# Attention and FFN with split fp32: four engines' order of work in front of the output projection

## The chip, the cores and the metric

The kernel runs on one core of one Trainium2 chip. The metric is device time in microseconds, the median of several executions. TensorE does the matrix products, ScalarE activations and copies, VectorE elementwise work, GpSimd some elementwise work and DMA issues, SyncE only DMA issues. Each runs its own list of instructions strictly in order and meets the others through semaphores.

## The reference

The input is `x` of 2048 rows by 1024 and a context of the same shape, seen as four batches (C = 4) of 512 rows (T = 512).

```python
def _L0_xattn_ref(query, key, value, mask, Wq, Wk, Wv, Wo):     # 32 query heads, 8 key/value heads, size 128
    q = (query @ Wq).reshape(b, t, h, d)
    k = (key @ Wk).reshape(b, t, kv_h, d)
    v = (value @ Wv).reshape(b, t, kv_h, d)
    q = apply_rope(q)
    k = apply_rope(k)
    logits = jnp.einsum('btkgd,bTkd->bkgtT', q, k) * ATTN_MULT
    logits = MAX_ATTN_VAL * jnp.tanh(logits / MAX_ATTN_VAL)
    logits = jnp.where(m, logits, -1e+30)
    weights = jax.nn.softmax(logits, axis=-1)
    attn = jnp.einsum('bkgtT,bTkd->btkgd', weights, v)
    return attn.reshape(b, t, h * d) @ Wo
...
x = x + xattn(_layernorm(x), ctx, ctx, mask, Wq, Wk, Wv, Wo)
x = x + ffn(_layernorm(x))                                      # base product, router with top 2 of 8, low-rank experts
```

The batches of the kernel's attention are the 16 sequences of 128 rows, four of them side by side in each c; a head group g is one of the 8 key/value heads with its four query heads.

## The kernel before, in words

Every fp32 operand of a large product is split into a high part of the type fp32r and a low part, and a product is three matmuls (helper `three`, lines 235 to 237): high by high, low by high, high by low. The split is one copy on ScalarE (the names end in `h`) and one subtraction on VectorE or GpSimd (names in `l`). The program has these stages, one behind the other: keys and values (K, V), queries (Q), attention with the output projection (O), and the feed-forward part. The last quarter of V (batch c = 3) is not projected in the K/V stage but in front of O, between the last query products and the first output products.

O is written as a schedule of steps `at`, from -16 to 255, eight steps for each of the 32 head groups `gi`. TensorE's `pe_att` (line 1257), ScalarE's `act_step` (1395), VectorE's `dve_step` (1494), GpSimd's `pool_step` (1580) and SyncE's `sp_step` (1687) each walk the steps, and in a step the order of the lines is the order on the engine. Tables say what falls into which step: `S_AT` scores, `DEN_AT` row sums, `ROWS_AT` the broadcast of reciprocals, `PV_AT` products of probabilities and values, `PL_AT` low parts of probabilities, `SPLIT` weight splits, `WL_AT` raw loads, `V_EVAC` copies of the value projection. Steps -16 to -1 are the front of O that this case is about; they lie at about 926 to 985 us.

The parts of one head group (four blocks b, numbered x = 4 gi + b):

- Query block x: `qf` is loaded by SyncE (`load_qk`), `qh` copied by ScalarE (`q_high2`, line 1374), `ql` subtracted by VectorE (`q_low2`, 1382). TensorE makes the scores of it; ScalarE applies tanh (1415), VectorE the mask's minimum (1545), ScalarE exp into `Pf` (1439) and the copy `Ph` (1441), VectorE the low part `Pl` (1567).
- Scores of block x write the same PSUM bank as those of x - 2, so they wait for exp of x - 2.
- Row sums: eight matmuls on ones (1300) into a bank, a copy `rT` (1393), a small transfer to `r` on 128 partitions (1604), the reciprocal on VectorE (1492), a small store to `rD` in DRAM (1588), and four broadcast loads into `RB` (1598), 256 KB each. The last three DMAs are issued by GpSimd.
- The product with the values waits for `Pl`. VectorE multiplies it by `RB` (1553), ScalarE copies it to `Ah` (1426) and VectorE forms `Al` (1512), which the output products read.

A weight piece x of 128 by 1024 comes from a raw load of SyncE (line 1198, three buffers), a copy `Rh` on ScalarE (1225) and a subtraction `Rl` on VectorE (1230) into a ring of four; here the pieces 8 to 11 are the value weights, and 12 and up the output weights. The last value projection consists of eight blocks of 24 matmuls. Its results are copied and split like everything else (`v_high`, line 1475, and `v_low`, 1481): blocks 0 to 3 into the upper halves of `Ah` and `Al`, which are free until the second head group, blocks 4 to 7 into two staging buffers `stg`. From there GpSimd stores them to `vE` in DRAM (`v_store`, 1488); they are read only by the last eight head groups.

Semaphores are counted per name: `tick` raises one, `wait_ge` waits for the value a named event reached; `SAME` lets names that never overlap share one.

Of the kernel before, what the change touches and what calls it, by code (L numbers as in the profile page):

```python
# [16 lines left out]
T = 512  # L17
# [38 lines left out]
SHARED_DMA += [(f"d_qw{i}", [f"d_ks{i}" if i < 2 else f"d_vs{i // 2 - 1}{i % 2}"]) for i in range(6)]  # L56
SHARED_DMA += [(f"d_vp{i // 2}{i % 2}", [f"d_vc{i // 2}{i % 2}"]) for i in range(4)]
SHARED_DMA += [(f"d_rb{i}", [f"d_bx{i}"]) for i in range(4)]
SHARED_DMA += [(f"d_x1{k}", [f"d_xt{k}"]) for k in range(4)]
SAME = {x: name for name, of in list(SHARED.items()) + SHARED_DMA for x in of}  # L60


# [35 lines left out]
def program(nc, xT, xN, ctxT, gran, mask, bias, cst, dram, out):  # L98
    kD, vD, vE, qD, XcD, QSD, X2D, x1D, rD = dram
    ctx = ExitStack()  # L100
    with ctx:
# [124 lines left out]
        def f(ap):  # L226
            return ap.bitcast(F32)
# [994 lines left out]
        def w_high(t, x):  # L1222
            w_free(t, x)
            t.wait_ge(f"d_w{raw_of(x)}", x)
            t.e.activation(piece(x)[1], raw[raw_of(x)][:, :], ACT.Copy).then_inc(*t.tick("w_hi", x))  # L1225
# [115 lines left out]
        def a_war(t, gi):  # L1341

            if gi > 1:
                t.wait_ge("o_job", 8 * (gi - 2) + 7)
            elif gi:
                for n in range(4):
                    for x in range(2):
                        t.wait_ge(f"d_vp{n % 2}{x}", n)
            else:
                t.wait_ge("q_pe", (31, 6))  # L1350

# [43 lines left out]
        def act_step(t, at):  # L1395
            e = t.e
            if at == -10:
                sums_copy(t, at)
            if at == -16:
                q_high2(t, 0)  # L1400
                q_high2(t, 1)
            if at not in (-9, -6, -2):
                v_high(t, at)
            for x in SPLIT.get(at, []):
                if x not in (7, 8, 9, 11, 12):
                    w_high(t, x)
            if at == -10:
                w_high(t, 11)
            if at == -9:
                v_high(t, at)  # L1410
            for gi, b in S_AT.get(at, []):
                x = 4 * gi + b
                s = ps[sbank[x % 2]][:, :]
                t.wait_ge("a_s", x)
                e.activation(s, s, ACT.Tanh, scale=SCALE / CAP).then_inc(*t.tick("a_tanh", x))  # L1415
                if at != -12:
                    q_high2(t, x + 2 if at != -11 else 4)
            if at == -13:
                w_high(t, 7)
            if at in (-3, 4):  # L1420
                sums_copy(t, -2 if at < 0 else at)
            for gi, b in PV_AT.get(at, []):
                x, i = 4 * gi + b, gi % 2
                t.wait_ge("a_an", x)
                a_war(t, gi)
                e.activation(Ah[:, 4 * i:4 * i + 4, b * P:b * P + P], v4(ps[obank[x % 2]][:, :]), ACT.Copy).then_inc(*t.tick("a_ah", x))  # L1426
            if at not in (-10, -2, 4):
                sums_copy(t, at)
            if at == -7:
                v_high(t, -6)  # L1430
            if at == -3:
                w_high(t, 12)
                v_high(t, -2)
            for gi, b in S_AT.get(at, []):
                x = 4 * gi + b
                s = ps[sbank[x % 2]][:, :]
                t.wait_ge("a_min", x)
                p_free(t, x)
                e.activation(Pf[x % NP][:, :], s, ACT.Exp, scale=CAP).then_inc(*t.tick("a_exp", x))  # L1439
                t.wait_ge("a_exp", x)  # L1440
                e.activation(Ph[x % NP][:, :], Pf[x % NP][:, :], ACT.Copy).then_inc(*t.tick("a_ph", x))
                if at == -13:
                    w_high(t, 8)
                if at == -11:
                    w_high(t, 9)
                    q_high2(t, 5)
            if 1 <= at < 9:
                n = at - 1
                t.wait_ge("o_job", n)
                t.wait_ge("v_job", ("last", 3))  # L1450
                e.activation(Y[:, n, :], ps[ring_bank(n)][:, :], ACT.Copy).then_inc(*t.tick("y_first", n))  # L1451
            act_ln(t, at)

        V_EVAC = {-9: (0, 1), -8: (2,), -7: (3,), -6: (4,), -4: (5,), -2: (6,), 0: (7,)}

        def v_key(n):
            return ("half", n) if n < 3 else ("quarter", 3) if n == 3 else ("full", n - 4) if n < 7 else ("last", 3)
# [16 lines left out]
                    t.wait_ge("q_pe", (31, 6))  # L1474
                e.activation(v_place(n)[:, 0, :], ps[v_bank(n)][:, :], ACT.Copy).then_inc(*t.tick("v_vh", n))

        def v_low(t, at):
            e = t.e
            for n in V_EVAC.get(at, []):
                t.wait_ge("v_vh", n)  # L1480
                e.tensor_tensor(v_place(n)[:, 1, :], ps[v_bank(n)][:, :], f(v_place(n)[:, 0, :]), ALU.subtract).then_inc(*t.tick("v_vl", n))

        def v_store(t, at):
            for n in V_EVAC.get(at, []):
                half, b4 = n // 4, n % 4
                t.wait_ge("v_vl", n)
                for x in range(2):
                    t.e.dma_start(vE[x, b4][:, T * half:T * half + T], f(v_place(n)[:, x, :])).then_inc(*t.tick(f"d_vp{n % 2}{x}", n, 16))

        def row_sums(t, gi):  # L1490
            t.wait_ge(f"d_rt{gi % 2}", gi)
# [2 lines left out]
        def dve_step(t, at):  # L1494
# [3 lines left out]
                q_low2(t, 1)  # L1498
            if at not in (-9, -4, -2):
                v_low(t, at)  # L1500
            for gi, b in S_AT.get(at - 1, []):
                if at not in (-12, -11, -10, -3, -2):
                    q_low2(t, 4 * gi + b + 2)
            if at == -9:
                w_low(t, 11)
                row_sums(t, 0)
                v_low(t, at)
            for gi, b in PV_AT.get(at - 1, []):
                x, i = 4 * gi + b, gi % 2
                t.wait_ge("a_ah", x)  # L1510
# [13 lines left out]
            if at >= 9:  # L1524
# [9 lines left out]
                else:  # L1534
                    t.wait_ge("y_first", m)
                e.tensor_tensor(Y[:, m, :], ps[ring_bank(n)][:, :], Y[:, m, :], ALU.add).then_inc(*t.tick("y_add", n))  # L1536
            for x in [y for y in SPLIT.get(at, []) if at < 0 and y not in (5, 7, 8, 9, 10, 11, 12)]:
                w_low(t, x)
            if at == -15:
                w_low(t, 5)  # L1540
# [15 lines left out]
                w_low(t, 7)  # L1556
            if at == -11:
                q_low2(t, 4)
                w_low(t, 9)
                q_low2(t, 5)  # L1560
            for x in [y for y in SPLIT.get(at, []) if at >= 0 and at != 4 or y in (8, 10)]:
                w_low(t, x)
            for gi, b in PL_AT.get(at, []):
                x = 4 * gi + b
                t.wait_ge("a_ph", x)
                t.wait_ge("a_den", gi)
                e.tensor_tensor(Pl[x % NP][:, :], Pf[x % NP][:, :], f(Ph[x % NP][:, :]), ALU.subtract).then_inc(*t.tick("a_pl", x))
            if at - 1 in DEN_AT and at not in (-9, 5):
                row_sums(t, DEN_AT[at - 1])
            if 11 <= at < 19:  # L1570
# [9 lines left out]
        def pool_step(t, at):  # L1580
# [18 lines left out]
            if at in DEN_AT:  # L1599
# [2 lines left out]
                if gi > 1:  # L1602
                    t.wait_ge(f"d_rs{gi % 2}", gi - 2)
                e.dma_start(r16[gi % 2][:, :], rT[gi % 2][0:P:32, :]).then_inc(*t.tick(f"d_rt{gi % 2}", gi, 16))  # L1604
            v_store(t, at)
            pool_rows(t, at)
            pool_ln(t, at)

# [78 lines left out]
        def sp_step(t, at):  # L1687
# [2 lines left out]
                load_qk(t, 1)  # L1690
            for x in WL_AT.get(at, []):
                w_load(t, x)
            if at == -9:
                load_v(t, 1)
            if at in (2, 3, 5, 6):
                j = (2, 3, 5, 6).index(at)
# [17 lines left out]
        for x in range(RAW + 4, 12 + 133):  # L1714
            at = split_at(x - RAW)
            if x - RAW >= 12 + 128:
                at = NT - 6 + 2 * (x - RAW - 140)
            WL_AT.setdefault(at + 1, []).append(x)


        def sp_att_early(t, u):
# [576 lines left out]
```

## Time and profile before

| | us |
|---|---|
| median of three runs | 2129.25 |
| lowest, highest | 2128.1, 2129.94 |
| the profiled execution's own time | 2128.13 |
| its span | 2126.3 |

| engine | busy us | share |
|---|---|---|
| TensorE, matmuls | 2118.6 | 100% |
| VectorE | 1652.2 | 78% |
| ScalarE | 879.3 | 41% |
| GpSimd | 338.8 | 16% |

The granted clock of TensorE is full throughout (the page's digits are all 9, the stretches say 1.00). A matmul is listed with a duration of 0.39 us, but they are pipelined: without a wait one starts every 0.23 us. So TensorE's time is read from the starts. Idle time of the other engines costs nothing unless TensorE comes to wait for them. Where the list of waits names an engine, it gives the one whose semaphore came last.

### The profile page before, as it was taken

To read this page: it belongs to the slowest core of one execution; us is meant where nothing else is said; L and a number is where in the kernel's file an instruction comes from. 1 tells how busy PE (TensorE), PEld (TensorE's weight loads), DVE (VectorE), ACT (ScalarE), POOL (GpSimd) and SP (SyncE) were. 2 spreads that over 40 slices of the span, in tenths; PEclk is the share of its full clock that TensorE was granted. 3 is DMA by queue.
4 is the path that set the end of the run, shared out by engine and by line. 5 is a ranking of instruction groups with operands and counts; after the bars stand their busy time and mean duration, and the time that the engine had idled before them with its cause. 6 is when DMAs were issued, how large, how long until landed. Compare 5 with 4: busy or idle time off the path is not lost.

```text
span 2126.3 us, 26531 instructions
## 1 busy us (share of the span) xinstructions
PE 2118.6 (100%) x9429; PEld 1721.3 (81%) x9429; DVE 1652.2 (78%) x2387; ACT 879.3 (41%) x1353; POOL 338.8 (16%) x438
## 2 busy tenths in 40 slices
PE   9999999999999999999999999999999999999999
PEld 8888888888888888877777877777787777888887
DVE  6969759999986666677877888998999898856533
ACT  3323343222241111157555556655666566423211
POOL 0000025666350000003111111111111110100000
PEclk9999999999999999999999999999999999999999
DMA  8778667777685566679656666678557854596761
GB/s 314 244 247 287 237 208 303 277 282 267 258 320 210 211 216 212 219 249 314 226 190 197 232 238 198 198 257 290 199 171 264 295 197 153 191 359 247 283 248 61
DMA packets 198820, 508.52 MB, mean 239 GB/s; under 512 B 20896, under 2 KB 46624, under 8 KB 196640
## 3 DMA queue, kind: packets, MB, share of 16 engines
q1 hardware_dynamic: 172448, 424.43, 56.6%
q0 software_dynamic: 26240, 82.38, 11.6%
q8 instruction: 76, 1.25, 0.2%
q14 instruction: 56, 0.46, 0.1%
HBM read 357.26 MB, written 149.16 MB: 238 GB/s over the span
## 4 chain that ended last, share of the span: by engine, by line
PE 97%; DMA 1%; ACT 1%; DVE 0%; issue 0%; SPq 0%; ACTq 0%; DVEq 0%
PE pq L235 32%; PE pq L236 31%; PE pq L237 31%; PE pq L1300 1%; PE pq L1959 0%; PE pq L1958 0%; DMA raw<-gran 0%; DMA raw<-ctxT 0%; DMA RB<-rD 0%; DMA rD<-r 0%; PE pq L411 0%; ACT Rh L1225 0%; SPq L1122 0%; DVE Rl L1230 0%; ACT Pf L1439 0%
## 5 line engine op out<-in xcount | busy, mean ns | idle before, releaser
L235 PE MATMUL pq<-Ah,Rh 128*128 128x512 f32 x1024 | 399.0, 390 | 0.0
L237 PE MATMUL pq<-Ah,Rl 128*128 128x512 f32 x1024 | 398.5, 389 | 0.0
L236 PE MATMUL pq<-Al,Rh 128*128 128x512 f32 x1024 | 398.5, 389 | 0.0
L235 PE MATMUL pq<-Xq,qW 128*128 128x512 f32 x896 | 348.7, 389 | 0.5 <-issue 0.4
L236 PE MATMUL pq<-Xq,qW 128*128 128x512 f32 x896 | 348.6, 389 | 0.0
L237 PE MATMUL pq<-Xq,qW 128*128 128x512 f32 x896 | 348.5, 389 | 0.0
L1230 DVE TENSOR_TENSOR Rl<-raw,Rh 128x1024 fp32r<-128x1024 f32 x176 | 214.2, 1218 | 91.4 <-ACT Rh L1225 91.0
L1225 ACT ACTIVATE Rh<-raw 128x1024 fp32r<-128x1024 f32 x176 | 185.3, 1054 | 166.2 <-PE pq L237 128.2
L235 PEld LDWEIGHTS pq<-Ah,Rh 128*128 128x128 f32 x1024 | 192.2, 188 | 41.9 <-ACT Y L1451 0.8
L237 PEld LDWEIGHTS pq<-Ah,Rl 128*128 128x128 f32 x1024 | 192.2, 188 | 40.5
L236 PEld LDWEIGHTS pq<-Al,Rh 128*128 128x128 f32 x1024 | 192.2, 188 | 40.1
L235 PEld LDWEIGHTS pq<-Xq,qW 128*128 128x128 f32 x896 | 168.2, 188 | 36.4 <-issue 1.3
L236 PEld LDWEIGHTS pq<-Xq,qW 128*128 128x128 f32 x896 | 168.2, 188 | 35.0
L237 PEld LDWEIGHTS pq<-Xq,qW 128*128 128x128 f32 x896 | 168.2, 188 | 34.6
L1536 DVE TENSOR_TENSOR Y<-pq,Y 128x512 f32<-128x512 f32 x248 | 169.4, 683 | 31.5 <-PE pq L237 31.2
L872 ACT ACTIVATE qW<-qraw 128x512 fp32r<-128x512 f32 x96 | 60.6, 632 | 293.3 <-PE pq L237 269.7
L1415 ACT ACTIVATE pq<-pq 128x512 f32<-128x512 f32 x128 | 74.6, 583 | 203.6 <-PE pq L237 203.5
L1604 POOL DMA_DIRECT2D r<-rT x32 | 22.6, 708 | 741.3 <-ACT rT L1393 718.3
L1545 DVE TENSOR_TENSOR pq<-pq,Bm 128x512 f32<-128x512 f32 x128 | 88.9, 695 | 64.9 <-ACT pq L1415 64.0
L1426 ACT ACTIVATE Ah<-pq 128x512 fp32r<-128x512 f32 x128 | 76.7, 599 | 94.3 <-DVE pq L1553 94.2
L235 PE MATMUL pq<-F,Rh 128*128 128x512 f32 x288 | 112.9, 392 | 0.0
L237 PE MATMUL pq<-F,Rl 128*128 128x512 f32 x288 | 112.2, 390 | 0.0
(243 smaller groups left out, 3935.2 us busy)
## 6 DMA issues: line engine op xcount, KB each, us to landing
raw<-gran SPq DMA_DIRECT2D x177, 512.0 KB, 4.4
QSD<-qW SPq DMA_DIRECT2D x64, 512.0 KB, 2.9
qD<-qt SPq DMA_DIRECT2D x128, 256.0 KB, 5.4
qW<-QSD SPq DMA_DIRECT2D x64, 512.0 KB, 3.4
qf<-qD SPq DMA_DIRECT2D x64, 512.0 KB, 6.1
RB<-rD POOLq DMA_DIRECT2D x128, 256.0 KB, 4.2
qraw<-gran SPq DMA_DIRECT2D x48, 512.0 KB, 5.2
kD<-kst SPq DMA_DIRECT2D x32, 512.0 KB, 5.7
```

Source lines behind the costliest of these rows:

```text
L235: e.matmul(dst, lh, rh, start=first, stop=False, skip_group_check=more)
L236: e.matmul(dst, lh, rl, start=False, stop=False, skip_group_check=more)
L237: return e.matmul(dst, ll, rh, start=False, stop=last, skip_group_check=more)
L872: e.activation(q_place(u)[:, 0, :], q_source(u), ACT.Copy).then_inc(*t.tick("q_hi", u))
L1225: t.e.activation(piece(x)[1], raw[raw_of(x)][:, :], ACT.Copy).then_inc(*t.tick("w_hi", x))
L1230: t.e.tensor_tensor(l, raw[raw_of(x)][:, :], f(h), ALU.subtract).then_inc(*t.tick("w_lo", x))
L1300: m = e.matmul(Tb[32 * y:32 * y + 32, :], f(ones[:, 0:32]), Pf[(4 * gi + y) % NP][:, :], start=True, stop=True, tile_position=(0, 32 * y))
L1415: e.activation(s, s, ACT.Tanh, scale=SCALE / CAP).then_inc(*t.tick("a_tanh", x))
L1426: e.activation(Ah[:, 4 * i:4 * i + 4, b * P:b * P + P], v4(ps[obank[x % 2]][:, :]), ACT.Copy).then_inc(*t.tick("a_ah", x))
L1536: e.tensor_tensor(Y[:, m, :], ps[ring_bank(n)][:, :], Y[:, m, :], ALU.add).then_inc(*t.tick("y_add", n))
L1545: e.tensor_tensor(v4(s), v4(s), bc(Bm[:, :].unsqueeze(1), [P, 4, P]), ALU.min).then_inc(*t.tick("a_min", x))
L1604: e.dma_start(r16[gi % 2][:, :], rT[gi % 2][0:P:32, :]).then_inc(*t.tick(f"d_rt{gi % 2}", gi, 16))
```

## The change

All of it is in the order of work in the steps -13 to -3.

- ScalarE: in step -10 the split of weight piece 11 moves behind the tanh and the query copy; in step -11 query copy 5 goes ahead of weight piece 9; value blocks 0 and 1 are copied in the order 1, 0.
- VectorE: the low part of query block 5 goes ahead of weight piece 9; weight piece 10 ahead of the minimum; weight piece 11 ahead of query block 6; and value block 0 is subtracted behind `Pl` 0, block 1 ahead of it.
- GpSimd: the stores of value blocks 0 to 3, which stood ahead of and behind the broadcast of the first head group, all move to step -3, behind the staging stores of blocks 4 and 5. They get semaphores of their own (`d_vf`, shared with `d_x1`), and the wait of `Ah` of the second head group (`a_war`) now names these.
- SyncE: raw loads 12, 13 and 14 move to the steps -7, -6 and -5, and the second value load from step -9 to step -5.

```diff
-SHARED_DMA += [(f"d_x1{k}", [f"d_xt{k}"]) for k in range(4)]
+SHARED_DMA += [(f"d_x1{k}", [f"d_xt{k}", f"d_vf{k // 2}{k % 2}"]) for k in range(4)]
...
@@ a_war
-                        t.wait_ge(f"d_vp{n % 2}{x}", n)
+                        t.wait_ge(f"d_vf{n % 2}{x}", n)
@@ act_step
-            if at == -10:
-                w_high(t, 11)
             if at == -9:
                 v_high(t, at)
             for gi, b in S_AT.get(at, []):
...
             if at == -13:
                 w_high(t, 7)
+            if at == -10:
+                w_high(t, 11)
...
                 if at == -11:
+                    q_high2(t, 5)
                     w_high(t, 9)
-                    q_high2(t, 5)
...
-        V_EVAC = {-9: (0, 1), -8: (2,), -7: (3,), -6: (4,), -4: (5,), -2: (6,), 0: (7,)}
+        V_EVAC = {-9: (1, 0), -8: (2,), -7: (3,), -6: (4,), -4: (5,), -2: (6,), 0: (7,)}
...
-        def v_low(t, at):
+        def v_low(t, at, which=range(8)):
             e = t.e
-            for n in V_EVAC.get(at, []):
+            for n in [x for x in V_EVAC.get(at, []) if x in which]:
@@ v_store
-                    t.e.dma_start(vE[x, b4][:, T * half:T * half + T], f(v_place(n)[:, x, :])).then_inc(*t.tick(f"d_vp{n % 2}{x}", n, 16))
+                    t.e.dma_start(vE[x, b4][:, T * half:T * half + T], f(v_place(n)[:, x, :])).then_inc(
+                        *t.tick(f"d_v{'p' if n > 3 else 'f'}{n % 2}{x}", n, 16))
@@ dve_step
+            if at == -9:
+                w_low(t, 11)
             for gi, b in S_AT.get(at - 1, []):
                 if at not in (-12, -11, -10, -3, -2):
                     q_low2(t, 4 * gi + b + 2)
             if at == -9:
-                w_low(t, 11)
                 row_sums(t, 0)
-                v_low(t, at)
+                v_low(t, at, (1,))
...
-            for x in [y for y in SPLIT.get(at, []) if at < 0 and y not in (5, 7, 8, 9, 10, 11, 12)]:
+            for x in [y for y in SPLIT.get(at, []) if at < 0 and y not in (5, 7, 8, 9, 11, 12)]:
                 w_low(t, x)
...
             if at == -11:
                 q_low2(t, 4)
+                q_low2(t, 5)
                 w_low(t, 9)
-                q_low2(t, 5)
...
                 e.tensor_tensor(Pl[x % NP][:, :], Pf[x % NP][:, :], f(Ph[x % NP][:, :]), ALU.subtract).then_inc(*t.tick("a_pl", x))
+            if at == -9:
+                v_low(t, at, (0,))
@@ pool_step
-            v_store(t, at)
+            if at > -7:
+                v_store(t, at)
+            if at == -3:
+                for x in (-9, -8, -7):
+                    v_store(t, x)
@@ sp_step
-            if at == -9:
+            if at == -5:
                 load_v(t, 1)
...
-            WL_AT.setdefault(at + 1, []).append(x)
+            WL_AT.setdefault({12: -7, 13: -6, 14: -5}.get(x, at + 1), []).append(x)
```

VectorE, steps -11 to -9, before. `Rl_169`, `Rl_170` and `Rl_171` are the low parts of weight pieces 9, 10 and 11, `ql_153` and `ql_152` those of query blocks 5 and 6, `Ah<-pq` those of value blocks 0 and 1, `Pl_185` that of the first probabilities:

```order
L1382 TENSOR_TENSOR ql_152<-qf_163,qh_150 128x512
L1230 TENSOR_TENSOR Rl_169<-raw_172,Rh_165 128x1024
L1382 TENSOR_TENSOR ql_153<-qf_163,qh_151 128x512
L1545 TENSOR_TENSOR pq<-pq,Bm 128x512
L1230 TENSOR_TENSOR Rl_170<-raw_173,Rh_166 128x1024
L1382 TENSOR_TENSOR ql_152<-qf_163,qh_150 128x512
L1230 TENSOR_TENSOR Rl_171<-raw_174,Rh_167 128x1024
L1492 RECIPROCAL r_55<-r_55 128x16
L1481 TENSOR_TENSOR Ah<-pq,Ah 128x512 x2
L1567 TENSOR_TENSOR Pl_185<-Pf_192,Ph_178 128x512
L1481 TENSOR_TENSOR Al<-pq,Al 128x512
```

The same place on VectorE in the changed kernel:

```order
L1382 TENSOR_TENSOR ql_152<-qf_163,qh_150 128x512
L1382 TENSOR_TENSOR ql_153<-qf_163,qh_151 128x512
L1230 TENSOR_TENSOR Rl_169<-raw_172,Rh_165 128x1024
L1230 TENSOR_TENSOR Rl_170<-raw_173,Rh_166 128x1024
L1547 TENSOR_TENSOR pq<-pq,Bm 128x512
L1230 TENSOR_TENSOR Rl_171<-raw_174,Rh_167 128x1024
L1382 TENSOR_TENSOR ql_152<-qf_163,qh_150 128x512
L1493 RECIPROCAL r_55<-r_55 128x16
L1481 TENSOR_TENSOR Ah<-pq,Ah 128x512
L1569 TENSOR_TENSOR Pl_185<-Pf_192,Ph_178 128x512
L1481 TENSOR_TENSOR Ah<-pq,Ah 128x512
L1481 TENSOR_TENSOR Al<-pq,Al 128x512
```

Query block 5 moved ahead of weight piece 9, piece 10 ahead of the minimum, piece 11 ahead of query block 6, and `Pl_185` between the two value blocks.

GpSimd, first head group, before (`r_55` and `r_56` belong to head groups 0 and 1):

```order
L1604 DMA r_55<-rT_154 128x1x16
L1588 DMA rD<-r_55 128x16
L1488 DMA vE<-Ah 128x512 x4
L1598 DMA RB<-rD 128x512 x4
L1488 DMA vE<-Al 128x512 x4
L1488 DMA vE<-stg_176 128x512 x2
L1488 DMA vE<-stg_177 128x512 x2
L1604 DMA r_56<-rT_155 128x1x16
```

The same place on GpSimd in the changed kernel:

```order
L1608 DMA r_55<-rT_154 128x1x16
L1592 DMA rD<-r_55 128x16
L1602 DMA RB<-rD 128x512 x4
L1488 DMA vE<-stg_176 128x512 x2
L1488 DMA vE<-stg_177 128x512 x2
L1488 DMA vE<-Ah 128x512 x4
L1488 DMA vE<-Al 128x512 x4
L1608 DMA r_56<-rT_155 128x1x16
```

The four broadcasts now follow the store of the reciprocals directly, and the eight stores of `Ah` and `Al` stand together ahead of the small transfer of the second head group.

SyncE, raw loads 9 to 14 with the loads of head groups 1 and 2 among them, before (`qf_162` and `kT_146` are of head group 2):

```order
L1198 DMA raw_174<-gran 128x1024
L1198 DMA raw_172<-gran 128x1024
L1657 DMA qf_162<-qD 64x4x512 x2
L1662 DMA kT_146<-kD 64x2x512 x2
L1198 DMA raw_173<-gran 128x1024
L1678 DMA vT_149<-vD 128x2x512
L1198 DMA raw_174<-gran 128x1024
```

The same place on SyncE in the changed kernel:

```order
L1198 DMA raw_174<-gran 128x1024
L1665 DMA qf_162<-qD 64x4x512 x2
L1670 DMA kT_146<-kD 64x2x512 x2
L1198 DMA raw_172<-gran 128x1024
L1198 DMA raw_173<-gran 128x1024
L1198 DMA raw_174<-gran 128x1024
L1686 DMA vT_149<-vD 128x2x512
```

Queries and keys of head group 2 moved ahead of a raw load, and the value load behind the last of three.

## Rows read from the trace of the kernel before

**Rows 1.** The page, busy time of TensorE: us, share of the span, instructions.

```profile
PE 2118.6 (100%) x9429; PEld 1721.3 (81%) x9429; DVE 1652.2 (78%) x2387; ACT 879.3 (41%) x1353; POOL 338.8 (16%) x438
```

**Rows 2.** Waits of TensorE: waited for, us in total, times, longest.

```profile
PE pq L235 <- ACT Pf L1439: 1.4, 1, 1.4
PE pq L235 <- DVE ql L1382: 1.0, 1, 1.0
```

**Rows 3.** Two stretches: length, busy us (instructions) by engine, clock, DMA share, GB/s.

```profile
960.00:980.00 20.00, 18.63 (x85) 14.01 (x84) 12.59 (x22) 11.14 (x21) 8.35 (x16) 1.00 1.02 366
1020.00:1820.00 800.00, 800.00 (x3602) 635.98 (x3601) 706.25 (x1071) 485.95 (x763) 110.34 (x196) 1.00 0.65 218
```

**Rows 4.** Timeline of TensorE, steps -9 and -8: start, duration, instruction, idle before.

```profile
952.27 0.40 PE L237 MATMUL pq<-qh,kT 128*128 128x512 f32 x1
953.69 0.50 PE L235 MATMUL pq<-qh,kT 128*128 128x512 f32 x1 [1.02 <-DVE ql L1382]
954.03 0.39 PE L236 MATMUL pq<-ql,kT 128*128 128x512 f32 x1
...
958.38 0.39 PE L237 MATMUL pq<-Rh,Vl 128*128 128x512 f32 x1
958.81 0.50 PE L235 MATMUL pq<-Rh,Vh 128*128 128x512 f32 x1
```

**Rows 5.** Timeline of TensorE, step -3.

```profile
975.34 0.47 PE L235 MATMUL pq<-Ph,vT 128*128 128x512 f32 x1
975.65 0.40 PE L236 MATMUL pq<-Pl,vT 128*128 128x512 f32 x1
975.88 0.40 PE L237 MATMUL pq<-Ph,vT 128*128 128x512 f32 x1
977.65 0.47 PE L235 MATMUL pq<-qh,kT 128*128 128x512 f32 x1 [1.37 <-ACT Pf L1439]
```

**Rows 6.** Timeline of ScalarE around query block 5.

```profile
950.74 1.04 ACT L1225 ACTIVATE Rh<-raw 128x1024 fp32r<-128x1024 f32 x1
951.68 0.61 ACT L1374 ACTIVATE qh<-qf 128x512 fp32r<-128x512 f32 x1
```

**Rows 7.** Timeline of VectorE, the first reciprocal.

```profile
958.67 0.24 DVE L1492 RECIPROCAL r<-r 128x16 f32<-128x16 f32 x1
```

**Rows 8.** Timeline of GpSimd, the small transfer.

```profile
953.09 0.71 POOL L1604 DMA_DIRECT2D r<-rT  x1 [317.52 <-ACT rT L1393]
```

**Rows 9.** DMA issues, 950 to 972 us: count, KB each, median us to landing.

```profile
vE<-stg POOLq DMA_DIRECT2D x2, 256.0 KB, 9.0
r<-rT POOLq DMA_DIRECT2D x1, 8.0 KB, 4.8
```

**Rows 10.** Chain that ended last, 959 to 972 us: start, us, what.

```profile
959.21 5.64 DMA rD<-r
...
965.25 5.83 DMA RB<-rD
...
971.18 0.71 DVE pq L1553
```

**Rows 11.** DMA issues, whole run.

```profile
RB<-rD POOLq DMA_DIRECT2D x128, 256.0 KB, 4.2
...
r<-rT POOLq DMA_DIRECT2D x32, 8.0 KB, 2.3
rD<-r POOLq DMA_DIRECT2D x32, 8.0 KB, 3.7
```

**Rows 12.** Timeline of GpSimd's DMA issues, 968 to 982 us.

```profile
968.55 2.15 POOL L1488 DMA_DIRECT2D vE<-Al  x4
...
976.09 1.07 POOL L1488 DMA_DIRECT2D vE<-stg  x2 [4.33 <-DVE stg L1481]
981.12 0.71 POOL L1604 DMA_DIRECT2D r<-rT  x1 [3.96 <-ACT rT L1393]
```

**Rows 13.** Timeline of VectorE, the second head group's reciprocal.

```profile
989.41 0.24 DVE L1492 RECIPROCAL r<-r 128x16 f32<-128x16 f32 x1
```

More of the change, by code:

```diff
@@ L1558, in dve_step @@
                 q_low2(t, 4)
+                q_low2(t, 5)
                 w_low(t, 9)
-                q_low2(t, 5)
-            for x in [y for y in SPLIT.get(at, []) if at >= 0 and at != 4 or y in (8, 10)]:
+            for x in [y for y in SPLIT.get(at, []) if at >= 0 and at != 4 or y == 8]:
                 w_low(t, x)
```

## The prediction

> **What bounds the kernel now.** I read the page first, then the list of waits of TensorE, then stretches, then single instructions of the stretch that waits. The page has TensorE busy for 2118.6 of 2126.3 us [rows 1]. The change leaves its instructions and their order alone, so it can only give back what TensorE waits. In the list of waits there is little: 1.4 us for ScalarE's `Pf`, 1.0 us for VectorE's `ql` [rows 2]; what else it waits stands at the start and end of the program, which the change does not touch. A stretch of 800 us in the long stage O has 800.00 us of TensorE work, while 960 to 980 us has 18.63 of 20, with a DMA share of 1.02 [rows 3]. The granted clock is 1.00 in both, so it is no term.
>
> Where TensorE does not wait, a matmul starts every 0.23 us (975.65, 975.88 in [rows 5]); three make 0.68, six 1.36, twenty-four 5.44. A late start also costs the restart after it, which the list of waits does not count. Place one: the scores that start at 953.69 could have started at 952.27 + 0.23 = 952.50, 1.19 us sooner, and the next matmul comes 0.34 instead of 0.23 later, 0.11 more: **1.30 us**. Place two: the value projection steps from 958.38 to 958.81, 0.43 instead of 0.23, and I count the same 0.11 of restart: **0.31 us** [rows 4]. Place three: scores at 977.65 which could have followed 975.88 at 976.11, 1.54 and some 0.08 of restart: **1.62 us**. A fourth is too short for the list: 975.34 to 975.65 is 0.31, a restart of **0.08 us** behind a wait for `Al` [rows 5]. Together 3.31 us, the ceiling of a gain in this profiled execution.
>
> **Edit by edit.** Nothing is added or removed: the same activations, subtractions and transfers in another order.
>
> *Query before weight on ScalarE and VectorE (steps -11 to -9).* In place one TensorE waits for `ql` 5 (the low part of the sixth query block), whose high part ran on ScalarE only at 951.68, behind the weight copy `Rh` 9 of 0.94 us started at 950.74 [rows 6]. Swapped, `qh` 5 runs 950.74 to 951.3 and `ql` 5 (0.60 us) ends by 951.95, before 952.50. The 1.30 us goes. What is moved behind: `Rh` 9 ends at 952.2, `Rl` 9 (1.13 us) by 953.45; TensorE, now 1.3 us earlier, wants it at 952.50 + 0.68 + 1.36 = 954.54. `Rl` 10 goes ahead of a minimum: by 954.9, wanted at 955.90. `Rh` 11 now stands behind a tanh and a query copy, about 954.7 to 955.7, so `Rl` 11 ends about 956.95. It used to end just ahead of the reciprocal at 958.67 [rows 7], which is place two. TensorE wants it at 957.26. So the 0.31 us goes too, with 0.3 us of margin; at worst it stays.
>
> *The first reciprocal.* The row sums' small transfer leaves at 953.09 and takes 4.8 us [rows 8, 9]: it lands near 957.9, while VectorE came to the reciprocal at 958.67 because it was at work. Now `ql` 6 ends by 957.5, so the reciprocal runs at 958.0, 0.65 us earlier. Then value low part 1, `Pl` 0 and low part 0, 0.60 apart from 958.15: `Pl` 0 is there at 959.4, wanted at 957.26 + 1.36 + 0.68 = 959.30. I count 0.1 us of new wait. Ten operations of 0.60 from 959.35 close low part 4 at 965.35, wanted at 959.4 + 0.68 + 5.44 = 965.5: nothing. Were the small transfer 1 us slower, 1 us would be lost here; faster, the 0.1 goes.
>
> *Broadcast before stores on GpSimd.* This is place three. Its chain: `rD` 5.64 us from 959.21, `RB` 5.83 us from 965.25, product at 971.18 [rows 10], then in ScalarE's order `Ah`, a staging copy, tanh and exp up to 977.5. From the broadcast's landing (971.08) to the scores (977.65) are 6.57 us. GpSimd's issue of the four `Ah` stores costs nothing there, since it was over before `rD` landed; what they cost is in flight: 1 MB on the same queue ahead of `RB`, with the DMA engines full. Over the whole run `rD` takes 3.7 us and `RB` 4.2 us at the median [rows 11]. In the new order the four stores are gone, and SyncE's `qf` and `kT` (1.5 MB) are issued before a raw load that waits for `Rl` 9, instead of behind it. Between the two pairs (5.64 and 5.83; 3.7 and 4.2) I take 4.2 and 4.7, nearer to the median because both crowds leave. Issue of `rD` 958.55, landed 962.75; `RB` issued 963.15, landed 967.85; scores possible at 974.4. TensorE without its waits comes to them at 976.11 - 1.30 - 0.31 - 0.08 + 0.1 = 974.5. So all 1.62 us goes, without margin. Bounds: with the medians there is 0.9 us to spare; with the old pair the broadcast lands at 970.4 and the scores start at 977.0, a gain of 0.7 in all.
>
> Here the Trainium skill has a formula (DMA: Bandwidth & Descriptors, Anatomy of one DMA): about 2.0 us fixed plus bytes over 436 GB/s. By it `rD` would take 2.0 us and `RB` 2.6 us, and place three would be cleared with some 4 us to spare. The rows disagree on the size, 5.64 and 5.83 here and 3.7 and 4.2 at the median, so it is no part of the sum.
>
> *Value stores and raw loads later.* Eight stores of 256 KB now leave in one go behind a pair of staging stores. That pair stood at 976.09 and comes 3.2 us earlier with the broadcast: 972.9 to 973.95, and the eight, 0.54 us each, until 978.3. Behind them on GpSimd is the next head group's small transfer, at 981.12 before [rows 12]; its producer is 3.1 us earlier too, so it leaves at 978.3 instead of 978.0. Its reciprocal ran at 989.41 [rows 13], so it must land by 986.3: 8.0 us of room against 4.8 above. The new wait for these stores is at the next group's product copies, some 20 us later. The raw loads wait for their buffers anyway and are wanted after 978; the value load behind them later still. All free.
>
> Sum: 1.30 + 0.31 + 1.62 + 0.08 - 0.1 = 3.2; less 0.1 for the place without margin: **3.1 us**. The profiled execution took 2128.13 us (2126.3 of span and 1.8 around it): it becomes 2125.0. The median of the runs is 1.1 us above it, and I forecast in its terms: 2129.25 - 3.1 = **2126.1 us**. Behind about 1000 us everything is only shifted.
>
> **Rivals.**
> B, *the broadcast is as slow as before*: SyncE's loads made it slow, not the stores. For it: the DMA share of 1.02, and three raw loads and `vT` still fall between 953.5 and 958. Against: 1 MB of stores and 1.5 MB of queries leave. Gain 0.7: 2128.5.
> C, *the weights become the wait*: `Rh` 11 slips behind the tanh, which waits for TensorE; `Rl` 11 is late and the chain from the reciprocal with it. Place two stays and 0.6 us come on top: 1.30 + 1.62 + 0.08 - 0.6 - 0.3 of a place three not fully cleared = 2.1: 2127.2. For it: 0.3 us of margin only.
> D, *the stores hold back the next group's row sums*, the slow side. Before, four `Al` and two staging stores were issued from 968.55 [rows 12], and the last pair, issued until 971.2, took 9.0 us [rows 9]: 11.7 us for six, 1.9 us each. Ten from 972.9 at that pace end at 991.9, and the small transfer, behind them on the queue, 2.3 us (its median, [rows 11]) later at 994.2, not by 986.3: 7.9 us late, with VectorE standing in the reciprocal and the weights behind it. -3.1 + 7.9 = +4.8: 2134.1. It decides once the transfer takes 8.0 us from its issue, and is slower than before from 11.1 us on. Against it: that pace was measured among SyncE's loads, with two broadcasts in flight.
> For D the Trainium skill has a rule (same page, Two DMAs through the same engine are not ordered): descriptors of one queue start in order. By that rule the small transfer does stand behind the large ones; whether it must wait for their end no row of before shows.
>
> **How the numbers follow.** Forecast 0.60, B 0.20, C 0.13, D 0.07 (slower by over 0.2% in 0.04 of it). The forecast's own range is 2.6 to 3.3 us of gain, and about 0.8 us either way for the median of a few runs (three spread from 2128.1 to 2129.94): 2125.0 to 2127.4. For 8 in 10 I take in B and C, to 2128.8, and below 2124.7. 0.2% is 4.3 us, about what can be told from no change; it lies above the ceiling of 3.3. It is reached only if other executions wait a microsecond longer here than the profiled one, as their 1.1 us more would allow: faster 0.16, same 0.80, slower 0.04.
>
> **What would show it.** TensorE's list of waits without `ql` and `Pf`; scores at 952.5 and 974.5; `qh` 5 ahead of `Rh` 9; the first product on `RB` by 968.0 (after 969.5 B is right); `Rl` 11 ended by 957.2, or C; the second reciprocal near 986.3 and no gap of TensorE there, or D. I am wrong if TensorE waits over 0.5 us between 985 and 1030, or if the time moves by over 4.3 us.

## The result and the profile after

| | before, us | after, us |
|---|---|---|
| median (22 runs each, side by side) | 2129.44 | 2126.31 |
| lowest, highest | 2128.05, 2131.89 | 2124.47, 2131.09 |
| the profiled execution's own time | 2128.13 | 2125.62 |
| its span | 2126.3 | 2123.8 |

The ratio is 0.9985, with a 95% interval of 0.9979 to 0.9992: a gain of 3.1 us, with 1.7 and 4.5 as its ends. That is under 0.2%, as forecast, and the time is 0.2 us above the predicted one.

In this document "to the third row sums" is the time from the first row-sum matmul of head group 0 (L1300) to that of head group 3. It holds all that the change touches and nothing of the program's start. Before it is 1024.65 - 950.71 = 73.94 us, after 1022.15 - 951.53 = 70.62 us, **3.32 us** less. Behind that point the program is only shifted: from the row sums of head group 3 to the end of the span are 1101.65 us before and after (1101.65 to 1101.73 in all ten traces). The span shrank by 2.5 only, because the first row sum itself comes 0.82 us later in this execution, 951.53 instead of 950.71; that is made in the keys and values at the very start, which the change doesn't touch, and differs from one execution to the next (950.51 to 952.23 in the ten traces). So 0.8 us is to be taken off a time of after when it is set beside one of before.

TensorE's busy time on the page of after; it answers to [rows 1]:

```profile
PE 2118.4 (100%) x9429; PEld 1721.7 (81%) x9429; DVE 1653.3 (78%) x2387; ACT 879.0 (41%) x1353; POOL 337.7 (16%) x438
```

TensorE's list of waits, after (waited for, us in total, times, longest); it answers to [rows 2]:

```profile
PE pq L411 <- DVE sel L516: 1.5, 1, 1.5
PE pq L235 <- issue: 0.4, 1, 0.4
PE pq L235 <- DVE kRl L522: 0.2, 1, 0.2
```

`Pf` and `ql` are gone, and nothing took their place: of the three left, `sel` and `kRl` belong to the program's start and the 0.4 us to the query stage, ahead of the change. Two stretches, after, answering to [rows 3]:

```profile
960.00:980.00 20.00, 20.00 (x93) 15.62 (x92) 15.26 (x25) 14.09 (x26) 9.24 (x17) 1.00 0.83 288
1020.00:1820.00 800.00, 800.00 (x3602) 635.99 (x3601) 706.53 (x1071) 485.71 (x762) 110.54 (x197) 1.00 0.65 218
```

TensorE now fills 20 of 20 us in place of 18.63. The stage behind is what it was. TensorE's timeline, after, at the places one, two and three and at the one late start left; it answers to [rows 4, 5]:

```profile
953.09 0.39 PE L237 MATMUL pq<-qh,kT 128*128 128x512 f32 x1
953.32 0.40 PE L235 MATMUL pq<-qh,kT 128*128 128x512 f32 x1
...
957.87 0.39 PE L237 MATMUL pq<-Rh,Vl 128*128 128x512 f32 x1
958.10 0.39 PE L235 MATMUL pq<-Rh,Vh 128*128 128x512 f32 x1
...
974.87 0.39 PE L237 MATMUL pq<-Ph,vT 128*128 128x512 f32 x1
975.10 0.39 PE L235 MATMUL pq<-qh,kT 128*128 128x512 f32 x1
...
1000.45 0.39 PE L237 MATMUL pq<-Ah,Rl 128*128 128x512 f32 x1
1000.85 0.47 PE L235 MATMUL pq<-Ph,vT 128*128 128x512 f32 x1
1001.16 0.39 PE L236 MATMUL pq<-Pl,vT 128*128 128x512 f32 x1
```

The scores that waited follow at 0.23 us (953.32 and 975.10), and so does the value projection of place two (958.10, the seventh of the block's eight threes of matmuls, as 958.81 was before). The one late start left is 1000.85: 0.17 late and 0.08 of restart, 0.25 us. The same matmul was late before, in a place that the prediction didn't count:

```profile
1003.08 0.39 PE L237 MATMUL pq<-Ah,Rl 128*128 128x512 f32 x1
1003.36 0.47 PE L235 MATMUL pq<-Ph,vT 128*128 128x512 f32 x1
1003.66 0.39 PE L236 MATMUL pq<-Pl,vT 128*128 128x512 f32 x1
```

That is 0.05 late and 0.07 of restart, 0.12 us.

ScalarE and VectorE, after, answering to [rows 6, 7, 13]. In the first of two fences ScalarE has query block 5 ahead of the weight piece, and the exp for which place three waited:

```profile
951.45 0.61 ACT L1374 ACTIVATE qh<-qf 128x512 fp32r<-128x512 f32 x1
951.97 1.04 ACT L1225 ACTIVATE Rh<-raw 128x1024 fp32r<-128x1024 f32 x1
...
973.71 0.60 ACT L1439 ACTIVATE Pf<-pq 128x512 f32<-128x512 f32 x1
```

VectorE has the first reciprocal, `Pl` 0, the first product on `RB`, and the second reciprocal:

```profile
958.31 0.25 DVE L1493 RECIPROCAL r<-r 128x16 f32<-128x16 f32 x1
...
959.03 0.68 DVE L1569 TENSOR_TENSOR Pl<-Pf,Ph 128x512 fp32r<-128x512 f32 x1
...
967.98 0.70 DVE L1555 TENSOR_TENSOR pq<-pq,RB 128x512 f32<-128x512 f32 x1 [1.56 <-DMA RB<-rD]
...
986.20 0.24 DVE L1493 RECIPROCAL r<-r 128x16 f32<-128x16 f32 x1
```

VectorE still waits 1.56 us for `RB`, but the product is at 967.98 instead of 971.18. exp ends at 974.31, and the scores start at 975.10. Before, exp ended at 977.5 and the scores started 0.15 later; so they could have started at 974.46 here, and there is a margin of 0.6 us in this execution.

GpSimd's issues, after, answering to [rows 8, 10, 12]:

```profile
953.80 0.71 POOL L1608 DMA_DIRECT2D r<-rT  x1 [317.44 <-ACT rT L1393]
958.86 0.56 POOL L1592 DMA_DIRECT2D rD<-r  x1 [4.35 <-DVE r L1493]
964.54 2.15 POOL L1602 DMA_DIRECT2D RB<-rD  x4 [5.13 <-DMA rD<-r]
...
973.34 1.07 POOL L1488 DMA_DIRECT2D vE<-stg  x2 [5.55 <-DVE stg L1481]
974.40 2.13 POOL L1488 DMA_DIRECT2D vE<-Ah  x4
976.52 2.13 POOL L1488 DMA_DIRECT2D vE<-Al  x4
978.64 0.70 POOL L1608 DMA_DIRECT2D r<-rT  x1
```

How long these took to land, after (count, KB each, median us), from three windows: 953 to 968, the first broadcast alone, and 970 to 980 us. They answer to [rows 9, 10]:

```profile
r<-rT POOLq DMA_DIRECT2D x1, 8.0 KB, 4.5
rD<-r POOLq DMA_DIRECT2D x1, 8.0 KB, 5.4
...
RB<-rD POOLq DMA_DIRECT2D x1, 256.0 KB, 3.3
...
r<-rT POOLq DMA_DIRECT2D x1, 8.0 KB, 7.0
```

`rD` is hardly faster than before (5.4 against 5.64). The first `RB` is: 3.3 against 5.83. And the second group's small transfer, 8 KB behind ten stores, took 7.0 us: 978.64 + 7.0 = 985.64, while VectorE's order reaches the reciprocal at 986.20. That is a margin of 0.56 us.

### The profile page after: what moved, and what is told of

It is laid out like the page before. It is cut to its first block, busy times and chain, and to the rows that moved or that the text cites. A ratio compares the mean times of both kernels' runs of the same rounds, so it can differ in the third digit from the quotient of the medians.

```text
span 2123.8 us, 26535 instructions
## 1 busy us (share of the span) xinstructions
PE 2118.4 (100%) x9429; PEld 1721.7 (81%) x9429; DVE 1653.3 (78%) x2387; ACT 879.0 (41%) x1353; POOL 337.7 (16%) x438
## 4 chain that ended last, share of the span: by engine, by line
PE 99%; DMA 0%; DVE 0%; SPq 0%; ACT 0%; issue 0%
PE pq L235 32%; PE pq L236 32%; PE pq L237 32%; PE pq L1300 2%; PE pq L1967 0%; PE pq L1966 0%; DMA kraw<-ctxT 0%; SPq L687 0%; PE pq L432 0%; PE pq L1773 0%; PE pq L1774 0%; PE pq L433 0%; PE pq L1989 0%; PE pq L1982 0%; DVE Xl L522 0%; ACT Xh L476 0%
```

## The experiments

The question behind them: which of the three engines' edits brings the gain, do they add up, and how near is the slow side? "ADDITIVE" and "COUPLED" are two theories of how the places add up. "STORES" and "LOADS" name what made the broadcast slow. "QUEUE" and "FREE" say whether a small transfer waits for the stores ahead of it on its queue or not.

| kernel | to third row sums | less before | median | before beside it | ratio (95%) |
|---|---|---|---|---|---|
| before | 73.94 | | | | |
| after | 70.62 | -3.32 | 2126.31 | 2129.44 | 0.9985 (0.9979 to 0.9992) |
| e1: ScalarE's and VectorE's edits alone | 74.99 | +1.05 | 2129.79 | 2129.09 | 1.0004 (0.9995 to 1.0013) |
| e2: GpSimd's edit alone | 72.15 | -1.79 | 2128.23 | 2129.09 | 0.9999 (0.9990 to 1.0008) |
| e3: SyncE's edit alone | 73.79 | -0.15 | 2128.52 | 2129.09 | 0.9997 (0.9988 to 1.0006) |
| e4: all but SyncE's edit | 70.71 | -3.23 | 2126.20 | 2129.09 | 0.9987 (0.9978 to 0.9996) |
| e5: eight stores twice | 79.59 | +5.65 | 2135.15 | 2129.21 | 1.0029 (1.0018 to 1.0040) |
| e6: raw loads later still | 74.56 | +0.62 | 2129.73 | 2129.21 | 1.0005 (0.9995 to 1.0014) |
| e7: stores behind the small transfer | 72.50 | -1.44 | 2127.00 | 2129.21 | 0.9993 (0.9984 to 1.0002) |
| e8: e6 and e7 together | 77.94 | +4.00 | 2132.45 | 2129.21 | 1.0016 (1.0007 to 1.0025) |

Differences of under 2 us don't show in the medians with certainty (the intervals reach 1.4 us and more to each side), so what follows reads the traces, one execution each, and takes the medians as a check: they have the same order but for neighbours that lie less than 1 us apart in the trace.

### e1: compute alone

```diff
@@ act_step, against before
-            if at == -10:
-                w_high(t, 11)
...
+            if at == -10:
+                w_high(t, 11)
...
+                    q_high2(t, 5)
                     w_high(t, 9)
-                    q_high2(t, 5)
...
-        V_EVAC = {-9: (0, 1), -8: (2,), -7: (3,), -6: (4,), -4: (5,), -2: (6,), 0: (7,)}
+        V_EVAC = {-9: (1, 0), -8: (2,), -7: (3,), -6: (4,), -4: (5,), -2: (6,), 0: (7,)}
@@ dve_step: the same edits as in the change; pool_step and sp_step stay as before
```

> Only the edits of ScalarE and VectorE (query 5 ahead of weight 9, weights 10 and 11, value blocks in the order 1, 0); GpSimd and SyncE as before. Theory COUPLED (place three is set by the broadcast's landing, so what TensorE gains at places one and two it waits again there): places one and two cleared, the waits of ql gone, but the wait for Pf at the scores grows from 1.4 to about 2.2 us; RB takes 5.8 us as before; net gain 0.8 us (0.4 to 1.4), about 2128.6. Rival ADDITIVE (each place is worth its own wait): the wait for Pf stays at 1.4 us and the gain is 1.6 to 1.7 us.

Measured: no gain, 1.05 us more to the third row sums. `ql` is gone from TensorE's waits as intended, but place three has grown. TensorE's timeline of e1:

```profile
975.61 0.47 PE L235 MATMUL pq<-Ph,vT 128*128 128x512 f32 x1 [1.03 <-DVE Al L1513]
...
977.91 0.47 PE L235 MATMUL pq<-qh,kT 128*128 128x512 f32 x1 [1.38 <-ACT Pf L1439]
...
979.17 1.94 PE L1300 MATMUL pq<-Pf,ones 128*32 128x512 f32 x8
```

and two stretches of it:

```profile
975.00:978.00 3.00, 1.01 (x4) 0.60 (x5) 3.00 (x6) 2.97 (x7) 1.07 (x2) 1.00 1.03 412
978.00:982.00 4.00, 4.00 (x14) 1.50 (x15) 2.35 (x4) 3.41 (x7) 0.00 (x0) 0.57 1.03 407
```

From the first row sums to the scores at 977.91 are 977.91 - 951.29 = 26.62 us, against 977.65 - 950.71 = 26.94 before: of the 1.6 us of places one and two 0.3 is left. The broadcast took 7.2 us (from its issue at 964.24 to the product at 971.45), where I expected 5.8. Counted from the first row sum it was issued 1.6 us earlier than before, and the product came only 0.3 us earlier; why it took longer was not tested. So the date hardly moved, and TensorE came earlier and waited longer, now twice, for `Al` and for `Pf`. Then its clock stood at 0.57 for four microseconds: the eight row sums took 1.94 instead of 1.06 us, and from these scores to the row sums of head group 2 it is 23.35 us against 21.80, which is 1.55 us more. -0.32 + 1.55 is the +1.23 us there, of which +1.05 is left at the row sums of head group 3. So ADDITIVE falls and COUPLED holds in kind: a gain in front of a fixed date is paid back at the date. The size was worse than I expected, by the clock.

### e2: stores alone

```diff
@@ pool_step, against before
-            v_store(t, at)
+            if at > -7:
+                v_store(t, at)
+            if at == -3:
+                for x in (-9, -8, -7):
+                    v_store(t, x)
@@ a_war: waits for d_vf, as in the change; act_step, dve_step and sp_step stay as before
```

> Only GpSimd's edit: the eight value stores behind the broadcast and the staging stores. Theory STORES (1 MB ahead on the same queue made RB slow): RB from 5.8 to 3.5 us, it lands before 969.5, the wait for Pf is gone, the one for ql (1.0) stays; gain 1.7 us. Rival LOADS (SyncE's raw, qf and kT loads made it slow): RB stays near 5.8 us and the wait for Pf stays above 1 us; gain under 0.4 us.

Measured: `Pf` is gone from TensorE's waits and `ql` (1.2 us) stays, 1.79 us less. Broadcast and store of e2, 958 to 968 us:

```profile
RB<-rD POOLq DMA_DIRECT2D x4, 256.0 KB, 4.2
...
rD<-r POOLq DMA_DIRECT2D x1, 8.0 KB, 5.1
```

`RB` was issued at 965.82 and the product ran at 969.50, 3.7 us where before had 5.9 (965.25 to 971.18), with SyncE's loads in the old order. STORES holds for `RB`, and all traces bear it out: the first of the four broadcasts took 5.8, 5.8 and 7.1 us in the three kernels with the `Ah` stores ahead of it (before, e3, e1) and 3.3 to 4.2 us in the seven without. The gain itself is less certain: the medians have 0.9 us for it, with an interval that includes none.

### e3: loads alone

```diff
@@ sp_step, against before
-            if at == -9:
+            if at == -5:
                 load_v(t, 1)
...
-            WL_AT.setdefault(at + 1, []).append(x)
+            WL_AT.setdefault({12: -7, 13: -6, 14: -5}.get(x, at + 1), []).append(x)
```

> Only SyncE's edit: raw loads 12 to 14 and the second value load later, queries and keys of head group 2 earlier. STORES expects RB still above 5 us and rD about 5 us, a gain of 0 to 0.5 us, both waits of TensorE still listed. LOADS expects rD 4.2 and RB 4.7 us, the wait for Pf gone, gain 1.6 us.

Measured: `Pf` 1.4 and `ql` 0.9 us both stay; `rD` 5.6, `RB` 5.7 us, the product at 971.55; 0.15 us less. LOADS falls for the broadcast: the loads' new order does not speed it up.

### e4: all but the loads

```diff
@@ sp_step, against the changed kernel
-            if at == -5:
+            if at == -9:
                 load_v(t, 1)
...
-            WL_AT.setdefault({12: -7, 13: -6, 14: -5}.get(x, at + 1), []).append(x)
+            WL_AT.setdefault(at + 1, []).append(x)
```

> The changed kernel without SyncE's edit. If SyncE's part brings nothing by itself: the same as the changed kernel, no wait of ql or Pf, gain 3.1 to 3.3 us against before. If it is needed to make rD and RB fast enough for a TensorE that is 1.6 us earlier: rD 5.6 us and RB 4.5 us or more, the scores of step -3 wait again 0.5 to 1.5 us, gain 1.7 to 2.7 us.

Measured: 70.71 against 70.62 us, and a median 2.9 us below before's where after's is 3.1 below. `RB` took 4.8 us at the median, the product ran at 969.21, and one short gap of 0.34 us is left in place three. SyncE's edit is worth 0.1 us in this pair of executions, and by that gap 0.35 us at most.

The three parts alone sum to +1.05 - 1.79 - 0.15 = -0.89 us, together they bring -3.32. The compute edits are worth nothing or less without the broadcast, and 3.23 - 1.79 = 1.44 us with it (2.0 by the medians of e2 and e4): that is places one and two, of which the prediction had 1.61.

### e5: eight stores twice

```diff
@@ pool_step, against the changed kernel; vX is a DRAM buffer that nobody reads
             if at == -3:
                 for x in (-9, -8, -7):
                     v_store(t, x)
+                for n in (1, 0, 2, 3):
+                    for x in range(2):
+                        e.dma_start(vX[x, n % 4][:, 0:T], f(v_place(n)[:, x, :])).then_inc(...)
@@ a_war: the wait of Ah names the second set of stores
```

> The changed kernel with the eight value stores issued twice (the second time to a DRAM buffer that nothing reads), still ahead of the second head group's small transfer r. Theory QUEUE (rival D of the prediction: a small transfer waits for the large ones ahead of it on its queue): r is issued 4.3 us later and still takes 7 us or more, so it lands 4 to 9 us later than the 985.6 of the changed kernel, where VectorE takes the reciprocal only 0.5 us after the landing; TensorE waits 3 to 8 us in all before 1005, 2129 to 2134 us. Rival FREE (what counts is only the issue): r takes about 4.5 us from its issue near 983, lands at 987.5, 1.3 us late, and the time is 2127 to 2128.

Measured: +8.97 us over after to the third row sums, slower than before by 5.65. The chain that ended last in e5 (start, us, what):

```profile
973.65 5.33 POOL vE L1488 x10
978.98 4.25 POOL vX L1616 x8
983.23 12.51 DMA r<-rT
...
995.77 0.25 DVE r L1493
...
996.62 0.79 PE pq L235
```

and a stretch of it:

```profile
996.00:1002.00 6.00, 5.38 (x13) 4.22 (x14) 6.00 (x10) 1.81 (x4) 3.75 (x7) 0.50 0.43 116
```

FREE falls: 8 KB behind 18 stores took 12.5 us, and TensorE waited 6.23 us behind the reciprocal. The loss is larger than the 2129 to 2134 us I expected, a median of 2135.15. That it is the order of the queue, and not only full DMA engines, this run alone doesn't settle; e6 and e8 do. From the first of the stores to the transfer's landing are 995.74 - 973.65 = 22.1 us, 1.23 for each store; in after, with ten stores, 985.64 - 973.34 = 12.3 us, 1.23 for each as well. The rest of the 8.97 us is the clock of 0.50 behind the wait.

### e6: raw loads later still

```diff
@@ sp_step, against the changed kernel
-            if at == -5:
+            if at == -2:
                 load_v(t, 1)
...
-            WL_AT.setdefault({12: -7, 13: -6, 14: -5}.get(x, at + 1), []).append(x)
+            WL_AT.setdefault({12: -2, 13: -2, 14: -2}.get(x, at + 1), []).append(x)
```

> The changed kernel with raw loads 12 to 14 and the second value load behind the queries of head group 3, at about 970 us instead of 954 to 958. If these loads are what kept rD at 5.1 to 5.7 us in every kernel so far: rD 3.3 to 4 us, the first product on RB 1.5 to 2 us earlier after the reciprocal (8 us instead of 9.7), and no change of time (within 0.5 us), since TensorE does not wait there any more; a loss of up to 1 us if weight piece 12 comes late. If not: rD still above 5 us.

Measured: my "no change of time" was wrong, it is 3.94 us slower than after. What it was built for it shows. DMA issues of e6, 958 to 968 us and 968 to 982 us:

```profile
rD<-r POOLq DMA_DIRECT2D x1, 8.0 KB, 1.7
...
r<-rT POOLq DMA_DIRECT2D x1, 8.0 KB, 11.8
```

and its stretch 958 to 961 us:

```profile
958.00:961.00 3.00, 3.00 (x15) 2.46 (x14) 3.00 (x7) 2.32 (x5) 0.60 (x2) 1.00 0.01 3
```

With the DMA engines idle (share 0.01) `rD` takes 1.7 us; in after the share is 0.84 from 958.8 to 961.8 us and it takes 5.4. So it is the loads that moved, SyncE's raw loads and the value load, that slow `rD`, while the first `RB` takes 3.5 us here, no less than after's 3.3. The product came 8.0 us behind the reciprocal instead of 9.7, and it brought nothing, since after had a margin there. The loads then fell onto the stores: the second small transfer took 11.8 us. From the first store at 971.80 to its landing are 18.05 us, 1.8 for each of the ten stores instead of after's 1.23. VectorE waited 3.44 us in its reciprocal, and TensorE 1.6 for `Pl`, 1.3 for `Al` and 0.4 for `stg`.

### e7: stores behind the small transfer

```diff
@@ pool_step, against the changed kernel
                 e.dma_start(r16[gi % 2][:, :], rT[gi % 2][0:P:32, :]).then_inc(*t.tick(f"d_rt{gi % 2}", gi, 16))
+                if gi == 1:
+                    for x in (-9, -8, -7):
+                        v_store(t, x)
             if at > -7:
                 v_store(t, at)
-            if at == -3:
-                for x in (-9, -8, -7):
-                    v_store(t, x)
```

> The changed kernel with the eight value stores behind the second head group's small transfer r instead of ahead of it. QUEUE: r takes 3 to 5 us instead of 7.0, nothing else moves, since the reciprocal there waits for VectorE's order; time the same within 0.5 us. FREE: r 7 us as before, the same time.

Measured: the small transfer takes 2.3 us instead of 7.0, with the same order of loads on SyncE. By itself this doesn't tell a queue from full engines, since the DMA share is 0.47 while it is under way, against 1.03 in after. And "nothing else moves" was wrong: 1.88 us are lost against after in the traces (0.7 in the medians). DMA issues of e7, 976 to 996 us:

```profile
r<-rT POOLq DMA_DIRECT2D x1, 8.0 KB, 2.3
rD<-r POOLq DMA_DIRECT2D x1, 8.0 KB, 6.5
```

and TensorE's timeline of e7:

```profile
974.48 0.47 PE L235 MATMUL pq<-qh,kT 128*128 128x512 f32 x1 [0.23 <-ACT Pf L1439]
...
1001.72 0.47 PE L235 MATMUL pq<-Ph,vT 128*128 128x512 f32 x1 [1.40 <-DVE Al L1514]
```

The stores now stand ahead of `rD` of the second group, which was issued at 986.78, at after's time (986.74), and took 6.5 us instead of 4.5. `Al` came 1.4 us late by it, at the matmul that is the late one in after too. The reciprocal had no use for an earlier transfer, as VectorE's order reaches it only then.

The other 0.5 us was lost at place three (974.48), before this run's edit can act: the first `rD` took 6.3 us instead of 5.4. Up to there after, e5 and e7 run the same program, and from the reciprocal to the first product on `RB` they need 9.7, 9.9 and 10.9 us. So the margin of 0.6 us at place three is smaller than the spread between executions. e4's 10.9 us lies inside this spread too, and doesn't say what SyncE's edit is worth.

### e8: both

The edits of e6 and e7 together.

> Both of the last two edits together, a candidate for less than the changed kernel: at most the 0.3 us of the last short wait near 1000.9 can still be had in front of O, so 2126.0 to 2126.6 and no difference that can be measured; a loss of up to 1 us if the raw loads, now among the stores, come late.

Measured: my "no difference" was wrong. `rD` of the second group takes 8.9 us, `RB` 8.0, and TensorE waits 4.2 us for `Al`, with a clock of 0.50 behind that wait. It is 7.32 us slower than after: loads and stores meet at the second group's store and broadcast instead of at its transfer.

The transfer itself, with the stretch in which it is under way:

```profile
r<-rT POOLq DMA_DIRECT2D x1, 8.0 KB, 5.4
...
978.60:984.00 5.40, 5.40 (x25) 4.48 (x24) 4.92 (x7) 5.34 (x8) 5.40 (x10) 1.00 1.04 396
```

This and e6 are the pair that settles QUEUE. SyncE's loads are the same and the DMA engines as full (share 1.04 here, 1.03 from 978 to 989.8 us in e6); only the eight stores stand behind the transfer instead of ahead of it, and it takes 5.4 us instead of 11.8. What is left with nothing but full engines is 5.4 us against e7's 2.3, some 3 us.

None of the eight is surely better than the changed kernel (e4's median is 0.1 us lower, well inside the intervals), and with 0.25 us of gaps left in front of O there was nothing worth building there.

## Why the prediction was right

The time, the class and the places came out as forecast. Two errors of the broadcast's sum cancelled, and one step, the stores, held by less than it reckoned: in both the agreement is partly luck. By its steps:

- **The ceiling.** 3.31 us at four places; the trace gave back 3.45 up to the row sums of head group 2 (48.74 against 45.29 us from those of group 0) and lost 0.13 net at 1000.85. The 0.14 above the ceiling are small late starts that it left out, such as 0.05 us at 975.34 (0.28 behind the matmul ahead of it). Forecast of 3.1, measured 3.3 in the trace and 3.1 by the medians. Why the late start at 1000.85 grew from 0.12 to 0.25 us was not tested.
- **Places one and two.** Both went, with `qh` 5 ahead of `Rh` 9 as worked out. C didn't happen: `Rl` 11 was over by 957.60 - 0.82 = 956.8, where 956.95 was forecast and 957.26 wanted (0.82 us is taken off for before's time). Their worth, 1.61 us, is 1.44 by e4 against e2, and nothing in e1: the prediction added them to place three without saying that they depend on it. It did set TensorE's arrival at place three 1.6 us earlier, which is the same dependence, but it counted the sum only for the whole change, where it holds.
- **The reciprocal.** Forecast 958.0, measured 958.31 - 0.82 = 957.5: the small transfer took 4.5 us instead of 4.8 and VectorE was free. The 0.1 us wait for `Pl` 0 did not come.
- **The broadcast.** Two terms of the sum were off, against one another. `rD` was taken at 4.2 and took 5.4 us; `RB` was taken at 4.7 and took 3.3 for the first. The reason given for 4.2, "because both crowds leave", fails for `rD`: one crowd, SyncE's raw loads, stays, and e6, where it is gone, has 1.7 us. For `RB` it is e2 against e3 that shows the cause: the stores ahead of it on its queue, 3.6 and 5.8 us for the first of the four. The product came at 967.2 in before's time, forecast by 968.0, and place three has a margin of 0.6 us where I saw 0.1; most of it is the reciprocal, 0.5 us earlier than forecast. That the two errors, 1.2 and 1.4 us, cancelled is luck. (With the medians of the whole run the prediction had 0.9 us to spare; its own terms give 1.1.) B was right that loads slow something, and wrong on what.
- **The stores in one go.** "8.0 us of room against 4.8" was the weakest step: it priced the transfer as if nothing stood ahead of it. It took 7.0, from its issue to the reciprocal were 7.6 us instead of 8.0, and the 3.2 us to spare were 0.56. That this edit cost nothing is nearer to luck than to the reckoning. D's mechanism is real (e5, and e6 against e8). What failed in D was its pace, 1.9 us a store: without broadcasts in flight ten take 1.23 each in after. With 1.23, ten stores from 972.9 end at 985.2, ahead of the 986.3 wanted. With the raw loads among them, in e6, it is 1.8, nearly D's. D's points of decision, 8.0 and 11.1 us, were about right: at 7.0 the change is good, and e6, with 11.8, is 0.6 us slower than before.
- **Loads later, "all free".** Right for what they cost (e3, e4: 0.1 to 0.35 us of gain), but not as a rule: e6 moves the same loads three to five steps further and costs 3.9 us.

Here the Trainium skill (DMA: Bandwidth & Descriptors, Anatomy of one DMA) has 2.0 us fixed plus bytes over 436 GB/s. With idle engines the run roughly agrees, 1.7 us for 8 KB in e6; under load the first `rD` takes 5.1 to 6.3 us in the eight kernels that keep loads beside it. The same page's rule that descriptors of one queue start in order (Two DMAs through the same engine are not ordered) agrees with e5 and with e6 against e8. What it is worth is in the measured 1.23 us for each store ahead, 1.8 with the raw loads among them.

## What to carry to other kernels

- A small transfer on the critical chain is priced by what stands ahead of it on its own queue: here 1.2 us for each 256 KB store, 1.8 with SyncE's loads among them, and with none ahead up to 3.7 us more where another queue has the engines full (`rD` at 1.7 and 5.4). Count the stores between its issue and the date at which its reader really comes to it, and move them only into a place where that sum fits, for every link of the chain and not just the first.
- Gains ahead of a date that a transfer sets are worth nothing until the date moves: measure edits together before dropping one that shows nothing alone.
- Work out the margin, not only the sum: here it was 0.6 us on both sides, less than one chain of transfers varied between executions of the same order (9.7 to 10.9 us), and each way of moving the stores or loads on lost 2 to 7 us.

## What was not expected of the hardware

TensorE's clock fell after waits, in kernels where the granted clock was 1.00 before. In e1 two waits of 1.0 and 1.4 us within 2.3 us are followed by a clock of 0.57 for 978 to 982 us, with single microseconds at 0.50, the lower of the two levels, 1.2 GHz. In e5 a wait of 6.23 us is followed by 0.50 until 1002, with a matmul every 0.43 us instead of 0.23, and in e8 one of 4.20 us likewise:

```profile
1006.00:1008.00 2.00, 1.66 (x4) 1.40 (x5) 1.93 (x3) 0.72 (x2) 0.00 (x0) 0.50 1.02 398
```

Before has waits of 1.0 and 1.4 us too, 24 us apart, and the clock stays at 1.00 [rows 2, 3]. So it does behind the single wait of 1.40 us in e7, and in e6 behind waits of 0.45, 1.55 and 1.32 us at 990.7, 995.3 and 1004.9. In before, e6 and e7 a wait cost what the list says and the restart, and in e1 1.55 us on top. Whether it is that two came close together was not tried.
